# One queue of PSUM banks, or banks by kind of product, in a decoder layer on one core

## The reference

```python
x = x + _L0_attn_ref(_layernorm(x, axis=-1), ...)   # qkv, rotary, 16 heads of 32, causal softmax, no projection
x = x + _L0_xattn_ref(_layernorm(x, axis=-1), ctx_2048, ...)
x = x + _L0_ffn_ref(_layernorm(x, axis=-1), ...)    # ternary weights: silu(gate) * up, RMS norm, down
```

## Time and profile before

| | |
|---|---|
| runs, median (lowest, highest) | 1302.16 us (1297.45, 1302.48) |
| profiled execution: its time, its span | 1296.46 us, 1294.4 us |
| TensorE busy, VectorE, ScalarE, GpSimd | 1188.4, 933.7, 798.9, 625.4 us |
| TensorE's share of the span | 92% |
| mean granted TensorE clock | 0.979 |

### The profile page before, as it was taken

The page is one execution under the profiler, slowest core; times in us unless marked ns, Lnnn a source line. Parts: engine busy times, 40 slices in busy tenths (PEclk is TensorE's granted clock), DMA queues, the critical chain, the costliest instruction groups (busy, mean ns, idle before and its releaser), DMA issues.

```text
span 1294.4 us, 19012 instructions
## 1 busy us (share of the span) xinstructions
PE 1188.4 (92%) x6266; PEld 787.2 (61%) x6312; DVE 933.7 (72%) x2714; ACT 798.9 (62%) x2301; POOL 625.4 (48%) x702
## 2 busy tenths in 40 slices
PE   5999997898999899999999999999999987998998
PEld 2667765565666666556655566666666655555545
DVE  5579998999888868877787855567778776563341
ACT  4675568687778766665766555666677656652230
POOL 2638975544534645545554531244445444263370
PEclk9998988899999999999999999999999999898999
DMA  8320000022202211123212300041101100000000
GB/s 256 98 89 11 2 1 1 1 66 66 66 3 65 89 57 64 51 81 106 89 42 88 106 24 29 13 155 45 57 13 58 57 17 1 1 1 8 23 1 29
DMA packets 25458, 65.58 MB, mean 51 GB/s; under 512 B 2720, under 2 KB 8992, under 8 KB 25360
## 3 DMA queue, kind: packets, MB, share of 16 engines
q1 hardware_dynamic: 25088, 64.00, 15.5%
q10 hardware_dynamic: 272, 0.36, 0.1%
HBM read 59.37 MB, written 4.98 MB: 50 GB/s over the span
## 4 chain that ended last, share of the span: by engine, by line
PE 44%; DVE 31%; ACT 17%; POOL 4%; issue 3%; DMA 1%; ACTq 0%; POOLq 0%; SPq 0%
PE ps L871 10%; PE ps L1072 8%; PE ps L1139 7%; ACT big L787 5%; PE ps L1188 4%; DVE big L987 4%; DVE big L414 4%; PE ps L1034 3%; PE ps L966 3%; DVE big L242 2%; PE ps L862 2%; DVE big L657 2%; DVE big L658 2%; ACT big L969 2%; PE ps L798 2%
## 5 line engine op out<-in xcount | busy, mean ns | idle before, releaser
L871 PE MATMUL ps<-big 128*125 128x512 bf16 x1152 | 264.9, 379 | 4.7 <-ACT big L969 2.0
L661 POOL TENSOR_TENSOR big<-big 128x448 f32<-128x448 bf16 x96 | 103.2, 1075 | 245.7 <-DVE big L984 210.0
L787 ACT ACTIVATE big<-ps,big 128x128 f32<-128x128 f32 (+1 forms) x472 | 177.2, 458 | 56.3 <-POOL big L432 55.9
L871 PEld LDWEIGHTS ps<-big 128*125 128x125 bf16 x1152 | 155.1, 136 | 92.6 <-issue 8.3
L862 PE MATMUL ps<-big 128*128 128x512 bf16 (+1 forms) x654 | 161.0, 389 | 2.8 <-issue 1.0
L987 DVE TENSOR_SCALAR big<-big 112x112 f32<-112x112 f32 (+1 forms) x256 | 141.3, 573 | 6.8
L969 ACT ACTIVATE big<-ps,big 112x375 f32<-112x375 f32 x128 | 74.7, 583 | 112.5 <-DVE big L968 111.9
L431 POOL TENSOR_TENSOR big<-big 128x4 f32<-128x4 f32 (+1 forms) x118 | 34.9, 295 | 222.2 <-ACT big L426 222.0
L662 POOL TENSOR_TENSOR big<-big 128x448 bf16<-128x448 f32 x96 | 137.7, 1435 | 7.5
L966 PE MATMUL ps<-big 128*112 128x375 f32 x256 | 107.1, 500 | 18.4 <-ACT big L804 8.1
L1034 PE MATMUL ps<-big 125*128 125x224 f32 (+1 forms) x512 | 119.7, 356 | 1.9 <-DVE big L1016 1.4
(11 more groups left out here) (115 smaller groups left out, 2311.4 us busy)
## 6 DMA issues: line engine op xcount, KB each, us to landing
big<-in_ctx_t SPq DMA_DIRECT2D x32, 375.0 KB, 3.5
big<-in_w_s SPq DMA_DIRECT2D x16, 512.0 KB, 3.6
big<-in_w_p SPq DMA_DIRECT2D x16, 512.0 KB, 3.6
big<-in_w_x SPq DMA_DIRECT2D x16, 512.0 KB, 3.6
big<-in_w_g SPq DMA_DIRECT2D x16, 512.0 KB, 3.9
big<-in_w_d SPq DMA_DIRECT2D x8, 512.0 KB, 4.5
big<-in_w_a SPq DMA_DIRECT2D x8, 384.0 KB, 5.0
scr<-big SPq DMA_DIRECT2D x24, 128.0 KB, 1.7
```

The lines of the kernel that those rows point to most:

```text
L787: t = act(lambda e, j=j: e.activation(z[0:rows, 128 * j:128 * j + 128], bk[0:rows, 128 * j:128 * j + 128], ACT.Identity, bias=rr[0:rows, 4 ...
L871: t = pe(lambda e, k=k, s=s, u=u, n=n: e.matmul(bk[0:CK, :], cT[:, s, k, CK * c:CK * c + CK], w[:, u, k, col:col + 512], start=n == 0, sto ...
```

## The change

The one `Pool` becomes six, over the same eight banks:

| pool | banks | takes from it |
|---|---|---|
| `bM` | 0, 1 | `a_mm`, `p_mm` |
| `bX` | 2, 3 | `b_m`, `a_tr`, `a_tq`, `l_2`, `lnb_t` (called by `p_t`), `t_s6`, `f_1` |
| `bS` | 4 | `a_s0`, `t_s0` |
| `bP` | 5 | `a_s2`, `t_s2` |
| `bO` | 6, 7 | `a_s3`, `t_s3` |
| `bG` | none at first | `g_0`, `d_0` |

From the tick `g_start` on, banks are handed to `bG`: three at once, one four ticks later, one seven, and two twelve ticks later. All other lines of the diff replace `bank` by the pool of the table.

```diff
-        bank = Pool([(p[:, :], p[:, :].bitcast(BF)) for p in psum])
+        banks = [(p[:, :], p[:, :].bitcast(BF)) for p in psum]
+
+        def home(*which):
+            p = Pool(banks)
+            p.idle = [(i, []) for i in which]
+            return p
+
+        def give(src, dst, n):
+            for _ in range(n):
+                dst.idle.append(src.idle.pop(0))
+
+
+        bM, bX, bS, bP, bO, bG = home(0, 1), home(2, 3), home(4), home(5), home(6, 7), home()
...
         def t_s0(it):
...
-            bi, (bk, _), free = bank.take()
+            bi, (bk, _), free = bS.take()
...
-            bank.release(bi, te)
+            bS.release(bi, te)
...
             if tick == g_start:
                 free_at[0] = all_now()
+                give(bM, bG, 2)
+                give(bX, bG, 1)
+            if tick == g_start + 4:
+                give(bS, bG, 1)
+            if tick == g_start + 7:
+                give(bP, bG, 1)
+            if tick == g_start + 12:
+                give(bO, bG, 2)
```

More of the change, by code:

```diff
@@ L353, in b_m @@
                 return
-            bi, (bk, _), bf = bank.take()
+            bi, (bk, _), bf = bX.take()
             tm = pe(lambda e: e.matmul(bk, oneb, u["a"].bitcast(BF), start=True, stop=True),
@@ L358, in b_m @@
             u["tc"] = act(lambda e: e.activation(sc, bk, ACT.Copy), tm)
-            bank.release(bi, u["tc"])
+            bX.release(bi, u["tc"])
         def b_2(u):
@@ L481, in a_tr @@
             h1 = it["h1"]
-            bi, (bk, _), free = bank.take()
+            bi, (bk, _), free = bX.take()
             for k in range(4):
@@ L503, in a_mm @@
                 if n == 0:
-                    it[f"b{j}"] = bank.take()
+                    it[f"b{j}"] = bM.take()
                 bi, (bk, _), free = it[f"b{j}"]
@@ L555, in a_te @@
             te = act(lambda e: e.activation(qT, src, ACT.Copy), t, of)
-            bank.release(bi, te)
+            bX.release(bi, te)
             it[f"qT{j}"] = (oi, qT, te)
@@ L591, in a_s2 @@
             p = g["p"]
-            bi, (bk, _), free = bank.take()
+            bi, (bk, _), free = bP.take()
             for h in range(4):
@@ L606, in a_s2e @@
                 te = dve(lambda e: e.tensor_copy(pT[0:T], src), t, pf)
-            bank.release(bi, te)
+            bP.release(bi, te)
             g.update(pT=pT, pTi=i, tpT=te)
@@ L613, in a_s3 @@
             if c == 0:
-                it["ob"] = bank.take()
+                it["ob"] = bO.take()
             bi, (bk, _), free = it["ob"]
@@ L806, in lnb_t @@
                 bt["ready"] += [tf]
-            bank.release(bi, tf)
+            bX.release(bi, tf)
         def proj_items():
@@ L850, in p_mm @@
             w = hf["w"]
-            bi, (bk, _), free = bank.take()
+            bi, (bk, _), free = bM.take()
             n = 0
@@ L995, in t_s2 @@
             hl = it["hl"]
-            bi, (bb, _), free = bank.take()
+            bi, (bb, _), free = bP.take()
             rows, nn = (T, 2) if S else (CK, 3)
@@ L1028, in t_s3 @@
             if g % 2 == 0:
-                bt["ob"] = bank.take()
+                bt["ob"] = bO.take()
             bi, (bk, _), free = bt["ob"]
@@ L1058, in t_s4 @@
                            [it["tpv"], t_rsm], cfree)
-            bank.release(bi, t1)
+            bO.release(bi, t1)
             bt["tcat"].append(t5)
@@ L1134, in g_0 @@
             for which in range(2):
-                bi, (bk, _), free = bank.take()
+                bi, (bk, _), free = bG.take()
                 n = 0
@@ L1191, in d_0 @@
                     n += 1
-            ri, (rk, _), rfree = bank.take()
+            ri, (rk, _), rfree = bG.take()
             tr = pe(lambda e: e.matmul(rk[0:T, 0:1], acc[j][:, sl], cf[:, C_UNIT:C_UNIT + 1], start=True, stop=True),
@@ L1206, in d_1 @@
                 it["t"], it["t2"], x1tok[b])
-            bank.release(it["bi"], t)
+            bG.release(it["bi"], t)
             small2.release(it["si"], t)
```

23 lines of the change are left out of this document (11 added, 12 removed).

## The result

The changed kernel takes 1443.93 us (median of 4 runs, 1440.89 to 1444.37), the kernel before 1300.47 us beside it: a ratio of 1.11, 95% interval 1.107 to 1.113. It is slower by 143 us; the forecast was 1400 us. The profiled execution took 1443.94 us, its span 1441.9.

What follows compares the result with a forecast made beforehand. TensorE, busy 92% of the span, was taken to lose its lead through per-kind banks; 93 us of waits on 1296.46 gave 1389.5, scaled to the median 1395, plus 5 for clock: 1400 us, range 1340 to 1455.

Steps and rivals of the forecast that it cites:

- The case that I held likeliest: Whole kernel: TensorE's bank waits cost time in every batch, giving 1350 to 1420 us; chance 58%.
- rival 3: Clock falls in each context batch: 27 us more, 1427 us, near 1450 with the self-attention halves; chance 18%.
- the 1.8 us of S: Self-attention halves: q products wait for k's bank to be emptied; 1.8 us stays per batch, 25 us over 14.
- the 3.6 us of X0: First context half: products of k's first tile start 3.6 us late, waiting for L787 to empty their bank.
- predicted 46: First context half X0: a batch grows from 42.74 to 46 us, 3.5 us each, 24 us over seven batches.
- predicted 43: Second context half X1: k products 3.7 us late, 2.3 stays per batch; batch 43 us, 17 us in all.
- 93 us in the sum: All stages: 12 + 4 + 25 + 24 + 17 + 11 us of added time from bank waits.
- rival 1: Lead paid once: TensorE moves back once per stage, then keeps pace; 16 us, 1318 us; chance 18% with half-way cases.
- I add 5 us for some more stretches at the lower clock: Whole kernel: the forecast's allowance for the lower clock, 5 us, taking 1395 to 1400 us.
- 12 us and part of the 4 for changes of stage: First attention: single scores bank costs 1.5 us in each of 8 batches, 12 us; stage changes A-S0 and S0-S1, 4 us.
- 8.5 us for the products: FFN start: gate and up products begin with three banks, the fourth 2.2 us late, smaller waits after; 8.5 us.
- For the transpositions of the norm 2.5 us: Last norm: the fourth transposition f_1 waits 2.5 us for a bank that the second L1110 empties.

Runs made afterwards that it cites:

- m2_r5_fill2: Against a control (two projection banks, five shared, one unused): 14 idle matmuls into the unused bank before long-waiting k and v products; 1384.10 us, control 1411.68.
- o1: Against the changed kernel: one bank for output products in place of two, the freed bank unused until the FFN; 1452.84 us.
- sp_22211: Against the changed kernel: two banks for scores and one for output products; 1443.64 us.

## Why the prediction was right, and which step was mis-sized

**The range and the forecast.** 1443.93 us lie inside the range of 1340 to 1455. The case that I held likeliest, 1350 to 1420 (58%), did not come. What came is the larger form of rival 3 ("near 1450"), and the range holds it only since it was drawn to reach there.

**Waits per batch: right.** "Only TensorE's waits change", and the bank's last reader is late in each batch: the 1.8 us of S measured 1.70, the 3.6 us of X0 3.99 with the projections alone apart. With the clock held up, X0 takes 46.6 us a batch (predicted 46) and X1 42.4 (predicted 43), though in a kernel whose other kinds share five banks. All waits together, 93 us in the sum, are 72 us of idle time. That they return each batch, and are not paid once (rival 1, 1318 us), is shown by the batches of 51.0 us.

**The clock: the step that failed.** "I add 5 us for some more stretches at the lower clock" measured up to 75 us of longer busy time on the same matmuls. I had the mechanism as rival 3, and set it aside because at 314.40 a stretch with 2.21 of 3.40 us busy had kept the clock. That one row was too little to go by. In the same trace of the kernel before another stretch was as busy, and the clock fell behind it:

```profile
184.70:188.10 3.40, 2.27 (x21) 2.05 (x22) 3.26 (x8) 2.04 (x9) 2.69 (x4) 1.00 0.00 0
188.10:191.50 3.40, 3.31 (x13) 1.26 (x11) 3.02 (x11) 3.40 (x18) 2.72 (x4) 0.53 0.00 0
```

And the new waits leave TensorE less busy than either row: 0.56 of 2.25 us at 449.87, nearer to the row of 201.70, behind which the clock had fallen. The clock's price had to be added to the forecast, since the case with waits in every batch is also the one that meets the clock. Rival 3's own price for the context halves, 27 us, was too small for the changed kernel: its longer busy time in X0 and X1 is 36.8 us (24.7 and 12.1). Rival 3 counted one fall of 1.7 us a batch, and X0 has two, of 2.6 and 1.7 us (5.38 and 4.49 in place of 2.77 and 2.80). The 27.6 us of m2_r5_fill2 are another kernel's, with two fillers a batch in X0 and one in X1; that they are near to 27 is luck. The rule that the prediction cites from the Trainium skill (TensorE: Matmul & The Clock Gate, "A second HAM failure mode: psum-queue depth-cycling") agrees with this trace: short idles between groups, the clock between 1.00 and 0.50, and 5.38 in place of 2.77 us behind them.

**A: mis-sized.** 12 us and part of the 4 for changes of stage; measured 31. I took VectorE for the one that sets the pace and TensorE's lead for spare, since VectorE was busy 58.35 of 60 us in the earlier trace rows. But TensorE was nearly as full there (57.45), and VectorE's busy time is no fixed amount: between 40 and 180 us one L658 takes 843 ns in the mean, in the changed kernel (L670) 499. The same 60 us in the changed kernel:

```profile
120.00:180.00 60.00, 58.10 (x363) 43.31 (x362) 44.24 (x87) 32.31 (x131) 42.66 (x41) 0.89 0.00 1
```

VectorE is busy 44.24 us with 87 instructions in place of 93, while TensorE is busy 58.10 us with 363 in place of 387, at a clock of 0.89 in place of 0.94. So TensorE is the fuller one now, and VectorE waits for it. Its waits for TensorE in A, in the kernel before (window 40 to 212):

```profile
DVE big L577 <- PE ps L571: 4.8, 3, 3.4
DVE big L606 <- PE ps L594: 1.4, 1, 1.4
```

and in the changed kernel (40 to 240):

```profile
DVE big L589 <- PE ps L583: 29.3, 20, 7.6
DVE big L618 <- PE ps L606: 13.4, 7, 3.6
```

36 us more. The single bank of scores makes most of A's 31 us (19 between o1 and sp_22211, 21 with the scores alone apart). What lowered the clock in A from 0.93 to 0.85 while TensorE idled only 7 us more was not tried and stays open, though 23.8 of the 31 us are longer busy time; so does the clock's part of the loss in S.

**Scores in S and X: overlooked.** I asked only for the projections there. Set apart alone, the single scores bank costs 46 us from S to X1. In the changed split it did little harm beyond A, because it shelters the projections' waits (a second scores bank won nothing in X0, by o1 and sp_22211); a kernel with three projection banks would have been forecast too fast.

**Last norm and FFN:** 8.5 us for the products; 7.0 measured. For the transpositions of the norm 2.5 us; their wait is 10.3 us (L1112 for L1122), and was 7.8 (L1100 for L1091).

## What to carry to other kernels

Ask of each kind of product, batch by batch, whether the instruction that empties its bank has ended when TensorE comes back for it: a small difference, paid in every batch, is the price of splitting a queue. Where such waits leave TensorE little work between them, price the products behind them at the lower clock as well, as part of the forecast: here that was half of the loss. One row in which the clock was kept is no proof that it will be kept. Banks given to one kind are taken from the lead of the others, so a split must be judged on all of them (two, three and four banks for projections, with five, five and four for all others: 1412, 1320 and 1413 us).

## What was not expected of the hardware

Matmuls whose output nobody reads can pay for themselves: with 59 us of them in the waits, the kernel was 27.6 us shorter (1384.10 against 1411.68), and the stretches of the context halves shown above ran at a clock of 1.00 in place of 0.91 and 0.95. And one idle of 1.7 us has the lower clock behind it at one time and not at another: in S1 of the changed kernel the q products wait 1.69 or 1.70 us in five batches in a row, before 397.25, 416.65, 434.39, 452.12 and 471.53 us, and only behind the first and the fourth did they run at the lower clock (3.08 and 3.33 us in place of 1.90). What decides between them no run here shows.
